# First edge stage of a graph network: edge attributes of two tiles taken together, low-weight products over 64 rows each

## What is computed

```python
ei = jnp.concatenate([x[src], edge_attr], axis=-1)     # 256 + 64 columns
core = jnp.maximum(ei @ W1 + b1, 0.0) @ W2 + b2
gate = jax.nn.sigmoid(ei @ Wg + bg)
agg = jax.ops.segment_sum(gate * core, dst, num_segments=x.shape[0])
```

## Time and profile before

| | |
|---|---|
| time, median of 3 runs | 4358.07 us (4357.03 to 4358.71) |
| span of the profiled execution | 4602.8 us, 244.7 us above the median |
| TensorE busy | 84% of the span |
| VectorE busy | 65% |
| ScalarE, GpSimd busy | 46%, 46% |
| DMA | 509.09 MB, 111 GB/s on average |
| first edge stage in the trace | from about 150 to 1640 us |

### The profile page before, as it was taken

One profiled execution on the slowest core, in us unless ns is written; L12 is line 12 of the kernel. 1 busy time (PEld: TensorE's weight loads), 2 busy tenths in 40 slices (PEclk: granted clock), 3 DMA queues, 4 the chain that ended last, 5 costly groups with the idle time before them and its releaser, 6 DMA issues. The chain is left out here.

```text
span 4602.8 us, 88005 instructions
## 1 busy us (share of the span) xinstructions
PE 3885.9 (84%) x23733; PEld 3489.0 (76%) x23733; DVE 2976.4 (65%) x7006; ACT 2107.0 (46%) x4811; POOL 2125.1 (46%) x2102
## 2 busy tenths in 40 slices
PE   7899999999999988989995666667666699999993
PEld 6798898989889877987885655556556578888883
DVE  7698898989889876554332222222321488989888
ACT  3565565656556536763221000000000288989882
POOL 0455555555555501000006666666666167667671
PEclk9899999999999987999995555665655599999996
DMA  4466666656556610004443333333333123323225
GB/s 138 135 176 171 171 175 171 177 170 175 169 170 177 169 31 23 24 26 161 151 150 103 89 87 89 92 87 91 87 89 90 52 55 75 63 67 70 60 48 120
DMA packets 226998, 509.09 MB, mean 111 GB/s; under 512 B 51805, under 2 KB 94299, under 8 KB 220426
## 3 DMA queue, kind: packets, MB, share of 16 engines
q0 software_dynamic: 116736, 313.66, 24.7%
q1 hardware_dynamic: 106389, 187.30, 14.6%
q10 hardware_dynamic: 3679, 5.79, 0.4%
HBM read 434.08 MB, written 72.49 MB: 110 GB/s over the span
## 5 line engine op out<-in xcount | busy, mean ns | idle before, releaser
L685 POOL DMA_INDIRECT big<-table,e_idx x784 | 751.2, 958 | 1049.6 <-DVE e_idx L721 649.0
L356 POOL DMA_INDIRECT big<-table,e_idx x784 | 767.0, 978 | 856.9 <-issue 304.1
L703 PE MATMUL psum<-e_near_hot,big 128*128 128x64 f32 x3136 | 621.9, 371 | 377.6 <-issue 361.9
L703 PEld LDWEIGHTS psum<-e_near_hot,big 128*128 128x128 f32 x3136 | 616.7, 292 | 391.7 <-issue 386.7
L2191 POOL DMA_INDIRECT g_S<-gsrc,g_idx x512 | 588.8, 1150 | 274.8 <-issue 157.8
L748 DVE TENSOR_TENSOR big<-big,psum 128x128 f32 x196 | 56.6, 289 | 801.9 <-remote 489.6
L435 ACT ACTIVATE e_hT_hi<-psum 128x256 fp32r<-128x256 f32 x784 | 300.2, 383 | 593.9 <-PE psum L375 513.1
L468 DVE TENSOR_TENSOR big<-psum,big 128x512 f32<-128x512 f32 x784 | 539.4, 688 | 45.5 <-issue 22.8
L386 PE MATMUL psum<-e_w_hi,e_hT_hi 128*128 128x256 f32 x1568 | 509.8, 325 | 0.3 <-issue 0.3
L386 PE MATMUL psum<-e_w_hi,e_hT_lo 128*128 128x256 f32 x1568 | 443.7, 283 | 0.0
L386 PE MATMUL psum<-e_w_lo,e_hT_hi 128*128 128x256 f32 x1568 | 440.7, 281 | 0.0
(11 more groups left out here) (397 smaller groups left out, 9090.5 us busy)
## 6 DMA issues: line engine op xcount, KB each, us to landing
big<-in_attr_t SPq DMA_DIRECT2D x392, 128.0 KB
g_rest<-gpart SPq DMA_DIRECT2D x128, 256.0 KB
big<-table,e_idx POOLq DMA_INDIRECT x1568
table<-C SPq DMA_DIRECT2D x26, 896.0 KB
table<-n_rows SPq DMA_DIRECT2D x24, 896.0 KB
experts<-g_region SPq DMA_DIRECT2D x15, 560.0 KB
g_S<-gsrc,g_idx POOLq DMA_INDIRECT x512
table<-big SPq DMA_DIRECT2D x25, 224.0 KB
```

Of the source, the lines that this page charges most:

```text
L356: pool.indirect_dma_start(G[:, j % 2, q, :], None, table, bass.IndirectOffsetOnAxis(idx[:, j, q:q + 1], 0)).then_inc(s[f"G_in{j % 2}{q}"], 16)
L685: pool.indirect_dma_start(G[:, j % n, q, :], None, c.table1, bass.IndirectOffsetOnAxis(idx[:, j, q:q + 1], 0)).then_inc(s[f"G_in{j % n}"], 16)
L703: last = pe.matmul(acc[:, b, :], G[:, j % n, q, b * 128:(b + 1) * 128], onehot[:, q, :], start=q == 0 and (b == 0 or s is sems[1]), stop=q ...
```

## The change

A tile's attributes are taken in pairs. `attr_lo` writes the low part in partitions 64 to 127 for the even tiles of a super tile, and in partitions 0 to 63 for the odd ones, in two instructions of 64 x 256 elements. The products with `wb_hi` stay over 128 rows. Those with `wb_lo` take the high part alone, over 64 rows: partitions 0 to 63 for the even tile, 64 to 127 for the odd one. TensorE issues, at every even step, the two low products and then the two high ones, for tiles u+4 and u+5. Both banks have to be free for that, so the wait is now for `whole_row` of the tile before the pair. `z_bank`, `turned` and `core_out` are only names for what stood there before.

```diff
-            def edge_part(a):
+            def edge_parts(a):
                 k, u, i, sp_, j, q = a
+                if q % 2 == 1:
+                    return
                 if q == 0:
                     pe.wait_ge(s["attr_ready"], p * NSUP + sp_ + 3)
-                pe.wait_ge(s["zs_ready"], p * NET + i + 2 * SUP - 1)
-                tile = parts[:, j % 2, q * ET:(q + 1) * ET]
-                pe.matmul(c.ps[u % 2], tile, wb_hi[:, :], start=True, stop=False)
-                pe.matmul(c.ps[u % 2], tile, wb_lo[:, :], start=False, stop=True).then_inc(s["z_ready"], 1)
+                pe.wait_ge(s["zs_ready"], p * NET + i + 2 * SUP)
+                for n in range(2):
+                    half, cols = slice(n * DE, (n + 1) * DE), slice((q + n) * ET, (q + n + 1) * ET)
+                    pe.matmul(z_bank(u + n), parts[half, j % 2, cols], wb_lo[half, :], start=True, stop=False)
+                for n in range(2):
+                    cols = slice((q + n) * ET, (q + n + 1) * ET)
+                    pe.matmul(z_bank(u + n), parts[:, j % 2, cols], wb_hi[:, :], start=False, stop=True).then_inc(s["z_ready"], 1)
...
-                for ahead, part in ((2, turn), (-2, total), (0, core), (4, edge_part)):
+                for ahead, part in ((2, turn), (-2, total), (0, core), (4, edge_parts)):
...
             def attr_lo(sup, j):
                 dve.wait_ge(s["attr_rounded"], p * NSUP + sup + 1)
-                dve.tensor_tensor(parts[DE:2 * DE, j % 2, :], attr[DE:2 * DE, j % 2, :],
-                                  parts[DE:2 * DE, j % 2, :].bitcast(F32), ALU.subtract).then_inc(s["attr_ready"], 1)
+                for n in range(2):
+                    half = slice((1 - n) * DE, (2 - n) * DE)
+                    here, there = (x[half, j % 2, :].rearrange("p (r n e) -> p r n e", n=2, e=ET)[:, :, n, :] for x in (parts, attr))
+                    last = dve.tensor_tensor(here, there, here.bitcast(F32), ALU.subtract)
+                last.then_inc(s["attr_ready"], 1)
```

More of the change, by code:

```diff
@@ L293, in window, with z_bank, turned, core_out @@
             return FAR_WIN, far_hot, c.psum[:, 6:6 + KB, 0:FAR_WIN]
+        def z_bank(u):
+            return c.ps[u % 2]
+        def turned(u):
+            return c.ps[2 + u % 2][:, 0:D]
+        def core_out(u):
+            return c.ps[4 + u % 2][:, 0:D]
         parts = sb("attr_parts", [128, 2, ES], F32R)
@@ L374, in turn @@
                 for b in range(KB):
-                    last = pe.transpose(c.ps[2 + u % 2][:, b * 128:(b + 1) * 128], Z[:, u % SLOTS, b * 128:(b + 1) * 128],
+                    last = pe.transpose(turned(u)[:, b * 128:(b + 1) * 128], Z[:, u % SLOTS, b * 128:(b + 1) * 128],
                                         c.ident[:, :])
@@ L385, in core @@
                     for x, y in ((hi, w2_hi), (hi, w2_lo), (lo, w2_hi)):
-                        last = pe.matmul(c.ps[4 + u % 2][:, 0:D], x, y[:, b, :], start=False, stop=b == KB - 1 and x is lo,
+                        last = pe.matmul(core_out(u), x, y[:, b, :], start=False, stop=b == KB - 1 and x is lo,
                                          skip_group_check=True)
@@ L419, in seed @@
                 act.wait_ge(s["msg_ready"], p * NET + i + SLOTS - 1)
-                act.activation(c.ps[4 + u % 2][:, 0:D], b2[:, :], ACT.Copy).then_inc(s["seeded"], 1)
+                act.activation(core_out(u), b2[:, :], ACT.Copy).then_inc(s["seeded"], 1)
             def step(k, u):
@@ L435, in high @@
                 act.activation(hT_hi[:, u % SLOTS, :, :].rearrange("p b n -> p (b n)"),
-                               c.ps[2 + u % 2][:, 0:KB * 128], ACT.Relu).then_inc(s["h_rounded"], 1)
+                               turned(u), ACT.Relu).then_inc(s["h_rounded"], 1)
             def gates(a):
@@ L467, in whole_row @@
                 dve.wait_ge(s["gate_ready"], p * NET + i + 1)
-                dve.tensor_tensor(Z[:, u % SLOTS, :], c.ps[u % 2], G[:, j % 2, q, :], ALU.add).then_inc(s["zs_ready"], 1)
+                dve.tensor_tensor(Z[:, u % SLOTS, :], z_bank(u), G[:, j % 2, q, :], ALU.add).then_inc(s["zs_ready"], 1)
                 if q == 0 and not (isinstance(k, int) and sp_ + 2 >= NSUP):
@@ L481, in hidden_lo @@
                 dve.scalar_tensor_tensor(out=hT_lo[:, u % SLOTS, :, :].rearrange("p b n -> p (b n)"),
-                                         in0=c.ps[2 + u % 2][:, 0:KB * 128], scalar=0.0,
+                                         in0=turned(u), scalar=0.0,
                                          in1=hT_hi[:, u % SLOTS, :, :].rearrange("p b n -> p (b n)").bitcast(F32),
@@ L505, in message @@
                 dve.wait_ge(s["hot_used"], p * NET + i + 1)
-                dve.tensor_tensor(msg[:, u % 2, :], c.ps[4 + u % 2][:, 0:D], gate[:, u % SLOTS, :], ALU.mult).then_inc(
+                dve.tensor_tensor(msg[:, u % 2, :], core_out(u), gate[:, u % SLOTS, :], ALU.mult).then_inc(
                     s["msg_ready"], 1)
@@ L600, in _ @@
                 for n in range(2):
-                    last = pe.matmul(c.ps[4 + n][:, 0:D], c.ident[:, :], c.mix[:, 0, :], start=True, stop=True)
+                    last = pe.matmul(core_out(n), c.ident[:, :], c.mix[:, 0, :], start=True, stop=True)
                 last.then_inc(marked, 1)
```

## The result

| | before | after |
|---|---|---|
| time, median | 4358.39 us (4357.03 to 4360.94, 4 runs) | 4457.98 us (4457.23 to 4460.86, 4 runs) |
| ratio | | 1.0232, interval 1.0217 to 1.0246 |
| span of the profiled execution | 4602.8 us | 4456.3 us |

The change makes the kernel 99.6 us slower; 54 were forecast.

The account below looks back on a forecast made before the run. TensorE bounds the stage now; after the change a loop through TensorE and VectorE does: 7.445 + 0.07 attr_lo + 0.16 layout = 7.675 us against 7.40 in four tiles, +54 us, 4358 to 4412 us; range 4315 to 4490.

Parts of the forecast that it names:

- the loop: Dependences through TensorE and VectorE over four tiles in the first edge stage: 7.21 us before, 7.675 after, setting the pace.
- the forecast case: The loop sets the first edge stage's pace, layout costing nothing to 0.35 a pair: 4412 us (4380 to 4450), chance 0.45.
- the rival without overlap: Low products run one after the other: loop 7.91 us, 4458 us; chance 0.17 together with the full layout price.
- Low products side by side, 0.235 for both: Two 64-row edge products on TensorE overlap in one spacing, so a pair costs 0.705 us, 0.235 less.
- Layout, 0.16 a pair: Going over to half-array products and back on TensorE: 0.08 us a change, two changes a pair.
- the upper bound: Dearest layout change on TensorE, product before running out and weights loaded in the open: 0.35 a change, 0.70 a pair.
- TensorE's own work: TensorE's work in four tiles of the first edge stage falls from 7.40 to 7.25 us, below the loop.
- attr_lo, 0.07 more: On VectorE, two 256-element instructions replace one of 512 once in four tiles: 0.07 us more, bounds 0 and 0.14.
- The new wait at nothing: TensorE's wait for whole_row of the tile before the pair, one tile later than today: no cost, cover 0.09 us.
- What the profile would show: Four tiles at 7.6 to 7.7 us, TensorE's stage busy share below 95%, its hidden_lo wait over 100 us.
- The faster rival: Unprofiled loop is shorter, so TensorE's work sets the time: 4329 us, or 4266 with layout free; chance 0.25.
- point of decision: Loop links together 0.2 us shorter bring the loop under 7.25 only if layout costs nothing or little (7.515 without it).

Follow-up runs that it names:

- e1: The changed kernel's pair order and two attr_lo instructions, but all four edge products over 128 rows; 4430.0 us beside 4361.2 for the kernel before, ratio 1.0153.
- e5: The changed kernel with add_window one step later, away from attr_lo; 4650.4 us beside 4579.9 for the kernel before, ratio 1.0155.
- e6: The changed kernel with the second attr_lo instruction left out; 4635.5 us beside 4579.9 for the kernel before, ratio 1.0136.
- e7: Pairs with all four products over 128 rows and add_window one step later; 4610.6 us beside 4579.9 for the kernel before, ratio 1.0088.
- e3: The changed kernel with both low products on the same 64 rows and one attr_lo instruction; 4506.0 us beside 4361.2 for the kernel before, ratio 1.0326.
- e2: The kernel before, one tile at a time, with its low product over 64 rows and two attr_lo instructions; 4654.2 us beside 4361.2, ratio 1.0667.
- e4: The kernel before with attr_lo as two instructions and nothing else; 4366.5 us beside 4361.2, ratio 1.0014.
- e11: The changed kernel as it is, run again on the third chip; 4693.2 us beside 4605.3 for the kernel before, ratio 1.0182.

## Why the prediction was right or wrong

- *Direction and mechanism.* Right. The saved columns don't shorten the loop enough, since the whole pair stands in its even step; e1 shows it without any halves (+69 us), and e5, e6 and e7 by shortening it.
- *The number.* 99.6 us against 54 is too far off for the forecast case as it was bounded, +22 to +92 us: the layout cost a little more than its limit of 0.35. That the result falls on the 4458 us of the rival without overlap is chance: the 0.235 of a second low product and the 0.225 by which the layout was under-priced are nearly the same.
- *Low products side by side, 0.235 for both.* Right, by e3.
- *Layout, 0.16 a pair.* Mis-sized; this is the term that failed. It measured 0.385 in the changed kernel and 0.37 to 0.39 in e2. I took the row of a change between fp32 and fp32r products as the nearest; half of the upper bound, 0.35 a pair, would have been nearer. With 0.385 the forecast's loop is 7.445 + 0.07 + 0.385 = 7.90 us, 98 us over the kernel before, against 99.6.
  The Trainium skill's rule (TensorEngine Tiling (Array Packing), Key Properties) that a change of tiling mode drains TensorE fits e2, where the two changes of a tile cost 0.39 us; it names no price.
- *TensorE's own work.* I had it falling to 7.25 and said that it stays below the loop. It rose to 7.70, since 0.385 is more than the 0.235 saved. So even without the loop the change would have lost, 0.27 of the 0.51 us, about half, as e6 shows; and the direction would have come out right with the loop's account wrong: it alone proves little.
- *attr_lo, 0.07 more.* Right (0.08 in the loop; in e4, where it is nearly hidden, 5 us).
- *The new wait at nothing.* Right as far as the traces show: in e1 the pair starts 0.12 after the last core product, as it did before. The 0.06 to 0.09 us that e5 and e7 stay over the added loop lie in front of and in the transposes, not here.
- *What the profile would show.* Wrong for two signs. TensorE's busy share didn't fall below 95%, and the wait for hidden_lo didn't exceed 100 us. Durations with modelled ends run over the gaps; but by starts, too, TensorE's work of 7.70 is 97% of 7.94, and a gap of 0.21 in each of 196 super tiles is some 41 us. The signs went with a TensorE work of 7.25, which the dear layout filled up. Four tiles at 7.6 to 7.7 became 7.94.
- *The faster rival.* It rested on the timed runs being quicker than the profiled one. That gap was one of chips, not of the profiler: the span after is 1.7 us below its median. Its point of decision was also reckoned wrong: a loop of 7.515 that is 0.2 shorter is 7.315, still over 7.25, so 0.27 would have been needed, and 0.59 for the -92 us, whose TensorE work is 6.93.

## What to carry to other kernels

Half-array products pay only if what they save between two changes of layout is more than the changes cost: here 0.39 us for going over and back, against 0.235 for one pair of 512 columns. Two pairs between two changes would save 0.47, an estimate from the same numbers that no run here tried, and it leaves out what four tiles at once would do to the loop. Before an engine's work is cut or bunched, add up the loop of dependences through the engines with the bunch inside: a pair of tiles taken together puts both tiles' time in one link. And look for gaps of TensorE in the distance between starts, not in busy time.

## What was not expected of the hardware

A product over 64 rows holds the array as long as one over 128: in e3 a second one on the same rows adds 0.24 us, the distance of two full products in the kernel before. A second one on the other half adds nothing (0.42 us for both, 0.43 for one alone in e2). The cost of changing the layout isn't paid at the change alone: in e2, 0.105 of the 0.39 us comes one product later, between the high product and the transposes, both over 128 rows; why isn't shown. And the chips differ: the same kernel took 5.6% longer on one than on another (4605 and 4361 us), and the change cost 2.3% on the quicker one and 1.8% on the slower one. The stalls of this stage are a small part of it: in e11 the stage is 28 us longer than in the trace after, of 237 us between the spans; the rest lies in other stages and wasn't followed.
